# Moving the split expert weights, their pieces, the spare blocks and the scatter waits of a graph attention and expert kernel

## The reference

```
h = layernorm(x)
scores = (h @ Wq.T + bq) @ (key @ Wk.T + bk).T / 64          # 4096 x 4096
scores = scores * adj;  scores = where(|scores| < 1e-5, -1e9, scores)
x1 = x + (softmax(scores) @ (value @ Wv.T + bv)) @ Wm.T + bm
y = layernorm(x1)
gate = softmax(y @ Wg + bg); keep the two largest, divided by their sum
out = x1 + sum over the two experts e of gate_e * (y @ We[e].T + be[e])
```

## Time and profile before

| what | us |
|---|---|
| median of 3 runs (1908.07 to 1912.19) | 1911.39 |
| the profiled execution: its time | 1913.32 |
| its span, first to last instruction | 1911.6 |
| TensorE busy in the span | 1815.1 (95%) |
| VectorE, ScalarE, GpSimd busy | 1180.8, 736.7, 244.4 |

### The profile page before, as it was taken

How to read it: one execution, slowest core, us unless ns; L and a number is a source line. 1 busy time by engine, 2 the same in 40 slices (tenths; PEclk the granted TensorE clock), 3 DMA queues, 4 the chain that set the end, 5 groups by cost and what they waited for, 6 DMA issues and landing times.

```text
span 1911.6 us, 33551 instructions
## 1 busy us (share of the span) xinstructions
PE 1815.1 (95%) x8730; PEld 847.9 (44%) x8731; DVE 1180.8 (62%) x3104; ACT 736.7 (39%) x1429; POOL 244.4 (13%) x277
## 2 busy tenths in 40 slices
PE   8999999999999999999998999999999998789993
PEld 4444444444444444444444444444444443345551
DVE  2888766666666666666666666666666663445451
ACT  1444444444343333344433333344433332234331
POOL 1000000000000000000000000001000000334544
PEclk9999999999999999999999999999999999989997
DMA  6355456666666666666656655556565558998865
GB/s 198 111 180 193 165 137 146 156 155 156 160 158 154 161 153 153 155 154 161 154 141 169 148 135 136 132 132 143 137 144 136 137 110 194 281 249 164 177 100 77
DMA packets 436574, 296.47 MB, mean 155 GB/s; under 512 B 319026, under 2 KB 343602, under 8 KB 436531
## 3 DMA queue, kind: packets, MB, share of 16 engines
q1 hardware_dynamic: 388562, 228.25, 48.5%
q0 software_dynamic: 16736, 38.35, 10.2%
q10 hardware_dynamic: 31232, 29.38, 5.2%
HBM read 152.68 MB, written 67.72 MB: 115 GB/s over the span
## 4 chain that ended last, share of the span: by engine, by line
PE 55%; DVE 13%; DMA 11%; issue 9%; ACT 7%; ACTq 2%; SPq 1%; POOLq 1%; DVEq 1%; POOL 0%
PE ps L1341 11%; PE ps L1343 11%; PE ps L1342 11%; PE ps L1444 6%; PE ps L1445 6%; PE ps L1446 6%; DMA out<-val_region,tok_ids 6%; DVE work L1025 4%; ACT work L743 3%; DMA work<-q_scratch 2%; ACT work L751 2%; ACT work L756 2%; DVE work L1032 2%; PE ps L1350 1%; DMA slots<-work,slots_u 1%
## 5 line engine op out<-in xcount | busy, mean ns | idle before, releaser
L1341 PE MATMUL ps<-key_region,work 128*128 128x512 f16 (+1 forms) x1336 | 507.9, 380 | 9.9 <-DMA work<-q_scratch 7.9
L1342 PE MATMUL ps<-key_region,work 128*128 128x512 f16 (+1 forms) x1336 | 507.5, 380 | 0.0
L1343 PE MATMUL ps<-key_region,work 128*128 128x512 f16 (+1 forms) x1336 | 507.3, 380 | 0.0
L1444 PE MATMUL ps<-val_region,work 128*128 128x512 f16 x1024 | 389.6, 380 | 33.8 <-DVE work L1067 26.5
L1445 PE MATMUL ps<-val_region,work 128*128 128x512 f16 x1024 | 389.7, 381 | 0.0
L1446 PE MATMUL ps<-val_region,work 128*128 128x512 f16 x1024 | 389.5, 380 | 0.0
L743 ACT ACTIVATE work<-work 128x512 f32<-128x512 f32 x256 | 161.3, 630 | 571.8 <-DVE work L1025 571.6
L1025 DVE SCALAR_TENSOR_TENSOR work<-ps,r_cur,work 128x512 f32<-128x512 f32 x256 | 191.9, 750 | 162.7 <-PE ps L1343 148.7
L1047 DVE TENSOR_TENSOR work<-work 128x512 f16<-128x512 f32 x256 | 176.4, 690 | 107.4 <-ACT work L756 106.9
L751 ACT ACTIVATE work<-work,exp_bias 128x512 f32<-128x512 f32 x256 | 181.4, 708 | 94.8 <-issue 56.8
L1035 DVE CUSTOM_DVE_ANT_0 work<-work 128x512 f32<-128x512 f32 x256 | 177.3, 693 | 49.4 <-DVE work L1032 49.4
(11 more groups left out here) (155 smaller groups left out, 1565.8 us busy)
## 6 DMA issues: line engine op xcount, KB each, us to landing
work<-in_adj SPq DMA_DIRECT2D x256, 256.0 KB, 3.0
val_region<-slots SPq DMA_DIRECT2D x58, 257.0 KB, 4.8
work<-in_valueT SPq DMA_DIRECT2D x8, 1024.0 KB, 6.7
work<-in_x SPq DMA_DIRECT2D x8, 1024.0 KB, 5.3
work<-in_keyT SPq DMA_DIRECT2D x8, 1024.0 KB, 5.4
q_scratch<-work SPq DMA_DIRECT2D x8, 1024.0 KB, 5.1
work<-q_scratch SPq DMA_DIRECT2D x32, 256.0 KB, 3.0
work<-in_x SPq DMA_DIRECT2D x32, 256.0 KB, 3.0
```

What stands on the lines that cost most here:

```text
L1341: nc.tensor.matmul(bank, st[0], mv[0], start=(k == 0), stop=False)
L1342: nc.tensor.matmul(bank, st[0], mv[1], start=False, stop=False)
L1343: last = nc.tensor.matmul(bank, st[1], mv[0], start=False, stop=(k == n - 1))
L1444: nc.tensor.matmul(bank, st[0], mv[0], start=first, stop=False)
```

## The change

It has five parts.

1. *Where the split weights go.* Expert e's halves now take exactly the columns of key chunk e in all eight planes of the key region, instead of one eighth of it in one run; a row's 4 KB become four pieces of 1 KB. So expert e may be loaded when the last tile's scores of chunk e are done. Experts 0, 1 and 2 are loaded inside the last tile's step, 3 and 4 among its exponents, and 5, 6 and 7 at lead steps 0, 1 and 2.
2. *Pieces.* On ScalarE the first exponent now comes ahead of the store of the fourth piece (which moves into the next tile) and of the load of the first one; `piece_high` and `piece_low` of piece 0 move behind chunk 2 and the residual, those of 1 and 2 one place further back.
3. *SyncE.* In the last tile `turn_rows(T-2)` moves behind the transposes of chunks 5 to 7. Blocks 6 to 8 are loaded ahead of the wait for expert 1 and the last tile's `turn_rows`.
4. *Spare blocks first.* `tables` puts the spare blocks ahead of the real ones in each half; it takes 19 steps where it took 14. A spare block, and the block behind it, count as starts of a run.
5. *Scatter waits.* In the 48 middle steps a run's start waits only for the scatter two steps back, which is the one of the same half. Ahead of the middle, GpSimd waits once for the last three scatters.

The diff, cut to its core:

```diff
-        we = key_region[:, :].rearrange("p (e a h k o) -> p e a h k o", h=2, e=E, a=2, k=KC // 2)
+        we = key_region[:, :].rearrange("p (a h k e o) -> p e a h k o", h=2, e=E, a=2, k=KC // 2)
...
@@ SyncE
-            turn_rows(T - 2)
             for c in range(5, C):
                 turn_probs(T - 1, c)
+            turn_rows(T - 2)
...
             sp.dma_start(out_tiles[1][TH - 1], x1_out).then_inc(x1_stored, 16)
+            for st in lead[6:9]:
+                load_block(st)
             expert_ready(1)
             turn_rows(T - 1)
-            for st in lead[6:]:
+            expert_ready(2)
+            for st in lead[9:]:
                 load_block(st)
-            for e in range(2, E):
+            for e in range(3, E):
                 expert_ready(e)
...
@@ GpSimd
-                for back in range(1, BEHIND):
+                for back in (BEHIND // 2,) if st.middle else range(1, BEHIND):
                     if st.has(back):
                         pool.wait_ge(y_added[(st.first - back) % RING], first + (st.added(back) - 16))
...
             pool.wait_ge(tables_done, 2)
+            for back in range(1, BEHIND):
+                pool.wait_ge(y_added[(LEAD - back) % RING], Step(LEAD - back).added(0))
...
@@ ScalarE
+            def load_expert(e):
+
+                act.wait_ge(s_mm, (T - 1) * C + e + 1)
+                for a in range(2):
+                    nc.scalar.dma_start(we[:, e, a].rearrange("p h k o -> p (h k) o"),
+                                        we_dram[2 * e + a].rearrange("p h (k o) -> p (h k) o", o=D)).then_inc(we_loaded[e], 16)
...
+            def attend(t, routes, splits=False, stores=False):
+
+                last = isl(t, T)
+                exponent(t - 1, 0)
+                if stores:
+                    store_piece(t - 3, 3)
                 if splits:
                     load_piece(t - 2, 0)
-                for c in range(4):
+                for c in range(1, 4):
                     exponent(t - 1, c)
                 absolute(t, 0)
-                if splits:
-                    piece_high(t - 2, 0)
                 exponent(t - 1, 4)
                 absolute(t, 1)
                 for c in range(5, C):
                     exponent(t - 1, c)
+                absolute(t, 2)
+                if splits:
+                    piece_high(t - 2, 0)
+                if last:
+                    load_expert(0)
+                absolute(t, 3)
                 if splits:
                     store_piece(t - 2, 0)
                     load_piece(t - 2, 1)
...
                 if splits:
                     piece_high(t - 2, 3)
-                    store_piece(t - 2, 3)
...
-            act.wait_ge(s_mm, T * C)
-            load_expert(0)
             for c in range(C):
                 exponent(T - 1, c)
-                if c == 3:
-                    load_expert(1)
+                if c == 1:
+                    load_expert(3)
...
             split_rows(T - 2)
-            load_expert(2)
+            load_expert(4)
...
+                if st.first + 5 < E:
+                    load_expert(st.first + 5)
                 if st.first + 3 < E:
-                    load_expert(st.first + 3)
                     load_bias(st.first + 3)
...
@@ VectorE, tables
+                spare = nd[:, 0:1]
+                step(nc.vector.tensor_scalar(spare, blocks_f[1][:, Z + E - 1:Z + E], -1.0, float(BLOCKS), ALU.mult, ALU.add))
+                nc.vector.tensor_scalar(k_real[:, :], iota_k[:, :], spare, None, ALU.subtract)
+                step(nc.vector.tensor_scalar(blocks_f[0][:, Z:], blocks_f[1][:, Z:], spare, None, ALU.add))
...
+                step(nc.vector.tensor_scalar(is_spare[:, :], tab_f[:, 0, :], 0.0, None, ALU.is_lt))
+                step(nc.vector.tensor_scalar(tab_f[:, 0, :], tab_f[:, 0, :], 0.0, None, ALU.max))
...
-                step(nc.vector.scalar_tensor_tensor(run_start[:, :], tab_f[:, 1, :], float(E), run_start[:, :],
-                                                    ALU.is_ge, ALU.max))
+                step(nc.vector.tensor_tensor(run_start[:, 1:], run_start[:, 1:], is_spare[:, 0:BLOCKS - 1], ALU.max))
+                step(nc.vector.scalar_tensor_tensor(tab_f[:, 0, :], is_spare[:, :], float(DUMMY), tab_f[:, 0, :],
+                                                    ALU.mult, ALU.add))
...
@@ VectorE, attend
                 mask(t, 0)
-                if splits:
-                    piece_low(t - 2, 0)
...
                     residual(t - 2)
                     route_stats(t - 2)
+                if splits:
+                    piece_low(t - 2, 0)
...
                 times_adj(t, 6)
+                mask(t, 6)
                 if splits:
                     piece_low(t - 2, 2)
-                mask(t, 6)
```

53 lines of the change are left out of this document (28 added, 25 removed).

## The result

| | before | after |
|---|---|---|
| median of the runs (lowest to highest), us | 1911.79 (1908.07 to 1912.30, 4 runs) | 1886.61 (1882.06 to 1888.70, 4 runs) |
| the profiled execution: time, span | 1913.32, 1911.6 | 1882.06, 1880.0 |

The ratio is 0.9869 with a 95% interval of 0.9847 to 0.9892: faster by 25 us (1.3%), where 46 were forecast (1865.2 us, range 1855 to 1880). The profiled execution of after is its fastest, 4.5 us under its median, so the spans differ by 31.6 us and the medians by 25.2. The traces account for the 31.6.

What follows compares the result with a forecast made beforehand. TensorE, busy 95% of the span, was taken as the bound, so only its stalls and the end could be won. Terms -24.1 +1.8 +1.1 -5.0 -3.0 -17.0 = -46.2 us gave 1867.1, as median 1865.2 us, range 1855 to 1880.

Steps and rivals of the forecast that it cites:

- Part 1, pieces: Tiles 3 to 17: with pieces behind the residual, each of 15 tiles saves 1.61 us, 24.1 us in all.
- I take the tile without pieces as the model: Attention loop: tiles with pieces would fall from 43.71 us between residuals to the 42.10 of tiles without.
- What is late next: Tiles with pieces: piece 2's low half makes the softmax bias up to 0.42 us later, covered by 0.87 us left over.
- Part 2, first tables: Routing tables after the last piece: a later store and 5 more steps, hidden by nothing, cost 1.8 us.
- Part 3, transposes of the last tile: Last tile's products: transposes no longer behind the rows' save 5.0 of 7.0 us, bounds 2 and 7.
- The collision: Last scores: moved weight loads hold up transposes, two chunks lose 4.26 us each, 8.5 us, giving 1874; chance 0.12.
- 14 us of all engines are free: Last scores' window: DMA share 0.55 leaves 14 us of all engines; the moved 3 MB ask for 12, so loading is hidden.
- Part 4 and the second tables: First expert blocks: earlier weight loads save 3.0 us (bounds 0 and 6.9); the longer second tables cost 1.1 us.
- The slower rival: Weight loads: 1 KB packets costing as much as 4 KB ones take 79 us more engine time, giving 1917; chance 0.03.
- Spares hold the first blocks: First expert blocks: three long landings in a row delay the last tile's row scatters and SyncE's loads, +5 us, 1870; chance 0.08.
- Part 5, the end: Last expert blocks: spares first and same-half waits let GpSimd's last scatter come sooner, 17.0 us saved, bounds 12 and 17.7.
- The end stays: Kernel's end: GpSimd's backlog has another cause and returns, 12 of the 17 us are lost, giving 1877; chance 0.05.

Runs made afterwards that it cites:

- a_qearly: After, with SyncE's load of the next tile's queries moved ahead of the adjacency load that waits for chunk 7's product: 1879.99 us, 0.9835 of before.
- a_halfspare: After, with the first half's spare blocks at the end again and before's shorter table for that half: 1882.20 us, 0.9841 of before.
- b_end: Before, with only the spare blocks put first (longer tables) and the scatter waits for the same half: 1902.91 us, 0.9945 of before.
- b_both: Before, with the new order of pieces, spare blocks first and same-half scatter waits, but the weights' layout, loads and SyncE's order unchanged: 1885.51 us, 0.9867 of before.
- b_layout: Before, with only the weights' new columns (1 KB pieces), the loads at their old places: 1921.78 us, 1.0046 of before.
- c_two: After, with both the earlier queries' load of a_qearly and the first half's spares at the end as in a_halfspare: 1871.99 us, 0.9777 of before.
- c_old: b_both, with the earlier queries' load of a_qearly and the first half's spares at the end as in a_halfspare: 1869.46 us, 0.9768 of before.
- a_late: After, with expert 0 loaded behind chunk 6's absolute values in the last tile and experts 1 to 3 at its exponents 1, 3, 5: 1889.03 us, 0.9902 of before.
- a_wlate: After, with experts 5, 6 and 7 loaded at expert-block steps 1, 3 and 4 instead of 0, 1 and 2: 1887.76 us, 0.9853 of before.
- c_best: c_two, with experts 5, 6 and 7 loaded at steps 1, 3 and 4 as in a_wlate: 1867.61 us, 0.9752 of before.

## Why the prediction was wrong

(The parts are numbered as in the prediction.) The direction was right, and so were most of the places; the size was off by 21 us against the medians, 14.6 against the profiled pair (46.2 forecast, 31.6 found). Two steps failed. The loop without pieces was taken for a floor that only the residual sets (part 1, 5.9 us), and moving the weights was counted as a gain that could at worst be nothing (parts 3 and 4 together, 8.0 us forecast, nothing net found). A third term, the spares and the second tables, was put at 1.1 us and measures 4.7.

- **Part 1, pieces: 24.1 forecast, 18.2 found.** The step that failed is "I take the tile without pieces as the model". The check that followed it, "What is late next", followed the piece's 0.42 us along one path only, to the bias and the residual. The same rows also stand ahead of `times_adj` of chunk 7, of the adjacency load that waits for it and of the queries' load behind that on SyncE, and that path had no 0.87 us to cover it. a_qearly took the queries' load off that path: 42.19 us, 0.31 less, which leaves the 42.10 of the forecast all but met. The tile without pieces, taken as a floor, was itself held by that load: without it, it takes 41.69.
- **Part 2, first tables: 1.8 forecast, 2.9 found**, of which a_halfspare's shorter table takes back 1.3 at tile 18.
- **Part 3, transposes of the last tile: 5.0 forecast (2 to 7), 7.5 found between the two traces**, of which some 5 are the change's and the rest is the slow trace of before. The wait for the rows' transpose that was left, forecast at 2, is 1.79 us. I had read the stall, 12 slow matmuls with it, from the one trace of before. In b_end TensorE stands 4.34 us too but comes back at 0.39 us a matmul, and the other wait, 2.99 us in before and said to stay, is 0.53.
- **The collision, a rival at 0.12, happened, in part**: +2.7 us in the last full tile. Its place was right and its price too high (8.5 us). "14 us of all engines are free" was true (0.55 became 0.91), but the room in the window said nothing of the one small transfer that is queued behind a large one: a transpose and a residual load took 8.7 and 8.2 us to land there, where the medians in the loop are 3.5 and 3.0. The Trainium skill (DMA: Bandwidth & Descriptors, Issuing engines are not separate DMA queues) says that transfers run on the same 16 DMA engines and interleave, whichever engine started them; these traces agree, since SyncE's transfers came late behind ScalarE's.
- **Part 4 and the second tables: -3.0 + 1.1 forecast, +6.9 found, an error of 8.8 us.** It has two halves. b_end, with the tables and the spares but not the weights, already loses 4.7 us of the 6.9, and b_both 5.8; what is left for part 4 is +1.1 us where -3.0 was forecast. The step that failed there is its range, with 0 as the lower bound: I bounded the gain from both sides but let no loss in, although the change also cut each load's rows into four. These few us can't be split finely: the eight other kernels with the weights early lose 3.8 to 11.1 us to before in this stretch, and a_qearly, which differs from after only ahead of it, 10.2. The slower rival priced those pieces as engine time only (79 us). That was far off: the queue's share of engine time goes from 5.2% to 5.7% of the span for 6144 more packets, (0.057 x 1880 - 0.052 x 1911.6) = some 8 us of all engines. What they cost is ScalarE's time at the issuing instruction, 5.31 and 3.07 us where before had 1.6 at most, and b_layout shows that cost alone, with the loads at their old places: 9 us. In after the loads are earlier and most of it is hidden again by step 13. b_both shows the whole of what belongs to the weights, parts 3 and 4 with the collision: nothing net, where 8.0 us were forecast. This is the largest error.
- **Spares hold the first blocks, a rival at 0.08, is true in part**: b_end's last scaling is 4.7 us late, and I had charged "three waits for a landing" to GpSimd as if nothing waited for it. Its second scatter of the last tile's rows, issued at 1670.62 in before and at 1677.33 in b_end, and the loads of the middle blocks stand behind. That the spares cost time is shown by c_two; that they are the cause of these 4.7 us is not, since c_old loses as much in the same steps with the first half's spares at the end.
- **Part 5, the end: 17.0 forecast, 16.7 found**, and 16.4 in b_end alone. Following GpSimd step by step gave this to 0.3 us.
- **The end stays** and **slower than before** did not happen.

So three rivals to which I had given 0.30 together were not alternatives to the forecast: all three were partly true at once. Their measured parts (2.7, 5.9, and 4.7 less the 1.1 already charged) put the forecast at 1877.4, where my range all but ended, and what part 4 lacked (4.1) lay outside it. That the transposes' term was met is partly luck: 7.0 us of stall were read from one execution, slower in that tile than the four that are alike there. The upper end, 1880, was made out of one rival and two small ones.

What stays open: why c_two gains more over a_qearly than the stalls at tile 18 and GpSimd's additions explain, and what of b_end's 4.7 us is the spares, what the longer second table (c_two and c_old kept it) and what the wait for three scatters ahead of the middle. The spares and the scatter waits of the middle were never timed apart. A kernel without the marks of the spares at all wasn't tried, since the spares' additions would then race with one another. Single runs of one kernel spread over 4 to 13 us, so gains under 4 us between two kernels rest on single traces here, which themselves differ by 2 to 4 us in stretches that no change touches.

## What to carry to other kernels

When work is moved earlier, follow every queue that the delayed row stands in front of, not only the one whose wait you are removing: here 0.42 us on VectorE reached TensorE through a load on SyncE. Read a stall from more than one execution before putting a price on it. A tile that "doesn't wait" is a model only of the wait you are looking at, so ask what bounds it. And a transfer had three prices here, the DMA engines' time, the delay of small transfers behind it, and the issuing engine's own time; the sum held nothing for the last two.

## What the runs showed of the hardware

Issuing a load of 512 pieces of 1 KB took ScalarE 0.55 to 0.68 us, even with the DMA share at 0.91 (after, 1540 to 1576 us); one of 128 pieces of 4 KB took 0.33 to 0.46 us (before, ahead of 1626 us). With the share at 0.99 the first kind, and the bias loads behind it, held ScalarE for 3.1 to 5.1 us an instruction in after and b_layout, and for up to 6.0 us in a_late. Of the second kind, and its bias loads, none took over 2.2 us in any kernel (1.6 in before), with a window just as full. The loads landed late in both: in the full window the median from issue to landing was 10.0 us in before, 8.0 in b_layout and 12.9 in after. So what the small pieces alone add (b_layout against before) is not the landing but the standstill of the engine that issues. Spreading the same loads over more steps (a_wlate, c_best) brought the issue down to under 2 us, with the pieces unchanged.
